# Transposing the normalised rows tile by tile instead of by the piece, in a graph transformer kernel on one core

## What is computed

```python
for i in range(4):
    h = layernorm(x) * ln1_g[i] + ln1_b[i]
    q = softmax(heads(h @ Wq[i]) * scale, axis=-1)
    k = softmax(heads(h @ Wk[i]) * scale, axis=-2)      # over all nodes
    v = heads(h @ Wv[i])
    x = x + (q @ (k^T v)) @ Wo[i] + bo[i]
    h = layernorm(x) * ln2_g[i] + ln2_b[i]
    x = x + gelu(h @ W1[i] + b1[i]) @ W2[i] + b2[i]
...
messages = relu(concat(xn[src], edge_attr) @ gnn_W1.T + gnn_b1)   # 100,000 rows, summed by dst
```

## Time and profile before

| | before |
|---|---|
| median of 3 runs | 2482.8 us (2479.87 to 2484.0) |
| the profiled execution | 2484.0 us, its span 2482.2 us |
| mean granted TensorE clock | 0.92 of full speed |
| TensorE matmul busy | 2040.7 us, 82% of the span |
| VectorE busy | 1571.9 us, 63% |
| GpSimd busy | 1318.0 us, 53% |
| ScalarE busy | 947.3 us, 38% |
| L1086 transposes | 600 |
| L830 activations | 240: 120 of 375 columns, 120 of 250 |

### The profile page before, as it was taken

The page is one execution under the profiler, slowest core; times in us unless marked ns, Lnnn a source line. Parts: engine busy times, 40 slices in busy tenths (PEclk is TensorE's granted clock), DMA queues, the critical chain, the costliest instruction groups (busy, mean ns, idle before and its releaser), DMA issues.

```text
span 2482.2 us, 36733 instructions
## 1 busy us (share of the span) xinstructions
PE 2040.7 (82%) x10686; PEld 1658.3 (67%) x10686; DVE 1571.9 (63%) x3709; ACT 947.3 (38%) x1978; POOL 1318.0 (53%) x1112
## 2 busy tenths in 40 slices
PE   3369899998889999897999988799999673999920
PEld 2247677776767777676777767677777472899920
DVE  4667777776877777677777767777776457011135
ACT  1234444443444444343444444344444241333310
POOL 3165666666556666755666665566666200332255
PEclk9779899999999999999999999999999785999965
DMA  8632222224222222422222232232223330999943
GB/s 199 198 72 57 72 69 67 68 70 116 59 70 68 69 70 68 122 59 63 71 71 70 71 102 72 60 74 68 68 69 72 71 93 21 321 331 325 326 114 95
DMA packets 262788, 260.78 MB, mean 105 GB/s; under 512 B 150233, under 2 KB 195158, under 8 KB 262674
## 3 DMA queue, kind: packets, MB, share of 16 engines
q0 software_dynamic: 124672, 132.82, 21.9%
q1 hardware_dynamic: 133890, 126.67, 16.6%
q10 hardware_dynamic: 4112, 0.03, 0.1%
HBM read 229.85 MB, written 28.39 MB: 104 GB/s over the span
## 4 chain that ended last, share of the span: by engine, by line
PE 50%; DVE 17%; POOL 11%; DMA 8%; issue 6%; ACT 5%; SPq 3%; DVEq 0%; POOLq 0%; ACTq 0%
PE bank L1040 26%; POOL G L759 10%; PE bank L1173 5%; DMA G<-P_d,src_T 4%; PE bank L1256 3%; PE bank L1264 3%; PE bank L1034 2%; PE bank L359 2%; PE bank L367 2%; PE bank L360 2%; DVE hn L1381 2%; DVE z L407 2%; DVE zl L381 2%; ACT TT L830 2%; PE bank L1100 2%
## 5 line engine op out<-in xcount | busy, mean ns | idle before, releaser
L759 POOL DMA_INDIRECT G<-P_d,src_T x896 | 1152.5, 1286 | 743.8 <-DVE z L407 457.4
L375 ACT ACTIVATE zr<-z 125x512 fp32r<-125x512 f32 x448 | 274.7, 631 | 512.9 <-DVE z L407 511.0
L407 DVE TENSOR_TENSOR z<-bank,G 125x512 f32<-125x512 f32 x448 | 294.4, 687 | 242.2 <-PE bank L367 120.5
L1173 PE MATMUL bank<-TT,W_s 128*128 128x250 f32 (+1 forms) x1280 | 367.0, 438 | 3.6 <-ACT TT L830 3.6
L1040 PE MATMUL bank<-W_s,hid 128*125 128x256 f32 x1600 | 359.6, 379 | 0.0
L1040 PEld LDWEIGHTS bank<-W_s,hid 128*125 128x125 f32 x1600 | 292.9, 188 | 42.6
L1173 PEld LDWEIGHTS bank<-TT,W_s 128*128 128x128 f32 x1280 | 241.9, 195 | 103.7 <-issue 8.9
L381 DVE SCALAR_TENSOR_TENSOR zl<-z,zr 125x512 fp32r<-125x512 f32 x448 | 289.6, 688 | 6.6 <-ACT zr L375 6.6
L359 PE MATMUL bank<-zr,onehot 125*125 125x256 f32 x896 | 270.0, 333 | 18.3 <-DVE zl L381 18.3
L360 PE MATMUL bank<-zl,onehot 125*125 125x256 f32 x896 | 229.3, 286 | 0.0
L359 PEld LDWEIGHTS bank<-zr,onehot 125*125 125x125 f32 x896 | 172.3, 192 | 44.2 <-DVE onehot L394 17.6
(11 more groups left out here) (284 smaller groups left out, 3055.5 us busy)
## 6 DMA issues: line engine op xcount, KB each, us to landing
W_s<-in_L_ffn_w SPq DMA_DIRECT2D x64, 512.0 KB, 4.3
hid<-in_L_ffn_w SPq DMA_DIRECT2D x64, 512.0 KB, 4.4
G<-P_d,src_T POOLq DMA_INDIRECT x896, 4.2
W_s<-in_L_mix_W SPq DMA_DIRECT2D x8, 1024.0 KB, 9.9
aT<-attr_d SPq DMA_DIRECT2D x224, 31.2 KB, 2.7
slot_out<-yo SPq DMA_DIRECT2D x32, 128.0 KB, 4.0
slot_out<-eT SPq DMA_DIRECT2D x32, 128.0 KB, 3.8
attr_d<-hn SPq DMA_DIRECT2D x12, 246.1 KB, 4.0
```

The source lines that it names most:

```text
L375: nc.scalar.activation(zr[:, s, k, :], z[:, k, :], ACT.Relu).then_inc(r_done, 1)
L407: nc.vector.tensor_tensor(z[:, k, :], edge_bank[k][0:ET, :], G[:, ST * s + 2 * k:ST * s + 2 * k + 2, :].rearrange("p j d -> p (j d)"), ALU ...
L759: pool.indirect_dma_start(G[:, j, :], None, P_d[:, :], bass.IndirectOffsetOnAxis(ap=src_T[:, at:at + 1], axis=0)).then_inc(g_in[j], 16)
L1173: ins = pe.matmul(to[:, 0:(b - a) * T], W1_s[:, k, part], TT[:, k, TT_PIECES[pc]], start=k == 0, stop=k == KD - 1)
```

## The change

TensorE now transposes a tile at a time: unit j of the group holds both halves of tile j, two blocks of 125 columns in one bank (`tile_T`). A group makes GT = 5 units of two transposes each instead of 4 units of three or two. ScalarE empties a unit with two activations of 125 columns, one for each half because gain and shift differ, and counts `ring_act` once, after the second. So a group has 10 activations in place of 4. The number and the shapes of the transposes stay the same, only their order changes.

The waits follow. `queries` waits for its own tile (`u + j + 2`) and no longer for a whole piece. The first part of the feed-forward block waits for b tiles of its piece (`GT + b + 1`: three, then five). The counts of units in a group (RING_GA, RING_GB, RING_M) and all positions behind them are shifted. VectorE waits for the same events under new numbers.

```diff
-        LNU = 2 * KD
-        RING_GA, RING_GB = 4 + LNU + GT, GT + LNU + 2 * NF + LNU
+        RING_GA, RING_GB = 2 * GT + 4, 3 * GT + 2 * NF
...
-            def features(u, loc, gain, shift):
-
-                for pc, (a, b) in enumerate(PC):
-                    for k in range(KD):
-                        i = KD * pc + k
-                        act.wait_ge(ring_full, u + i + 1)
-                        act.activation(TT[:, k, TT_PIECES[pc]], RING[(loc + i) % 3][:, 0:(b - a) * T], ACT.Identity,
-                                       bias=shift(k), scale=gain(k)).then_inc(ring_act, 1)
+            def features(u, loc, j, gain, shift):
+
+                act.wait_ge(ring_full, u + 1)
+                for k in range(KD):
+                    ins = act.activation(TT[:, k, tt_cols(j)], RING[loc % 3][:, 128 * k:128 * k + T], ACT.Identity,
+                                         bias=shift(k), scale=gain(k))
+                ins.then_inc(ring_act, 1)
...
-                    features(u, loc, lambda k: ln_col(0, k), lambda k: ln_col(1, k))
+                    for j in range(GT):
+                        features(u + j, loc + j, j, lambda k: ln_col(0, k), lambda k: ln_col(1, k))
...
                 def normalised(h, u, loc):
-                    for pc, (a, b) in enumerate(PC):
-                        for k in range(KD):
-                            i = KD * pc + k
-                            to = slot(u + i, loc + i)
-                            for j in range(a, b):
-                                if k == 0:
-                                    pe.wait_ge(hn_done, h + j + 1)
-                                ins = pe.transpose(to[:, (j - a) * T:(j - a) * T + T], hn[:, j, 128 * k:128 * k + 128], ident[0:T, 0:T])
-                            ins.then_inc(ring_full, 1)
+                    for j in range(GT):
+                        pe.wait_ge(hn_done, h + j + 1)
+                        tile_T(u + j, loc + j, hn[:, j, :])
...
                     for j in range(GT):
-                        pe.wait_ge(ring_act, u + (KD + 1 if j < PC[0][1] else LNU + 1))
+                        pe.wait_ge(ring_act, u + j + 2)
                         row(r + j, rloc + j, [(TT[:, k, tt_cols(j)], Wq_s[:, k, :]) for k in range(KD)])
...
                             if f == 0:
-                                pe.wait_ge(ring_act, u0 + (GT + KD * pc + KD + 1))
+                                pe.wait_ge(ring_act, u0 + (GT + b + 1))
```

More of the change, by code:

```diff
@@ L342, in build @@
         EG_B = EG_M + 1
-        RING_M, ROW_M = LNU + NG * RING_GA, NG * ROW_GA
+        RING_M, ROW_M = GT + NG * RING_GA, NG * ROW_GA
         RING_B, ROW_B = RING_M + 1, ROW_M + GT + KD
@@ L877, in _ @@
                     eg = l * EG_L + g + (EG_FIRST + EG_A)
-                    u0, q0 = l * RING_L + g * RING_GA + (RING_A + LNU), l * (2 * NG) + g * 2
+                    u0, q0 = l * RING_L + g * RING_GA + (RING_A + GT), l * (2 * NG) + g * 2
                     for pc, (a, b) in enumerate(PC):
@@ L887, in _ @@
                     for j in range(GT):
-                        copy_tile(u0 + LNU + 4 + j, LNU + 4 + j, es[:, j, :].rearrange("p (k n) -> p k n", k=KD), 128, T)
+                        copy_tile(u0 + GT + 4 + j, GT + 4 + j, es[:, j, :].rearrange("p (k n) -> p k n", k=KD), 128, T)
                     edges(eg, 1)
@@ L907, in second @@
                     std(std5b[:, :], mv5b[:, :, 1], b_std)
-                    features(u0 + GT, GT, lambda k: ln_col(2, k), lambda k: ln_col(3, k))
+                    for j in range(GT):
+                        features(u0 + GT + j, GT + j, j, lambda k: ln_col(2, k), lambda k: ln_col(3, k))
                     step(0)
@@ L911, in second @@
                         for pc, (a, b) in enumerate(PC):
-                            loc = GT + LNU + 2 * f + pc
+                            loc = 2 * GT + 2 * f + pc
                             act.wait_ge(ring_full, u0 + loc + 1)
@@ L918, in second @@
                     if not last:
-                        normalised(u0 + GT + LNU + 2 * NF, GT + LNU + 2 * NF)
+                        normalised(u0 + 2 * GT + 2 * NF, 2 * GT + 2 * NF)
                     step(5)
@@ L1092, in _ @@
                     h0, q0 = l * HN_L + g * GT + (NT + GT), l * (2 * NG) + g * 2
-                    u0, r0 = l * RING_L + g * RING_GA + (RING_A + LNU), l * ROW_L + g * ROW_GA + ROW_A
+                    u0, r0 = l * RING_L + g * RING_GA + (RING_A + GT), l * ROW_L + g * ROW_GA + ROW_A
                     for pc, (a, b) in enumerate(PC):
@@ L1108, in _ @@
                         for j in range(a, b):
-                            loc = LNU + 4 + j
+                            loc = GT + 4 + j
                             pe.wait_ge(ring_act, u0 + (2 * pc + 3))
@@ L1120, in _ @@
                                 if h == 0:
-                                    pe.wait_ge(ring_act, u0 + (LNU + 4 + j + 2))
+                                    pe.wait_ge(ring_act, u0 + (GT + 4 + j + 2))
                                     pe.wait_ge(row_dve, r0 + j + 2)
@@ L1139, in _ @@
                 pe.wait_ge(wQ_in, l * 32 + 32)
-                queries(uM - GT - LNU, rM, 0)
+                queries(uM - GT, rM, 0)
                 pe.wait_ge(ring_act, uM + 2)
@@ L1163, in second @@
                     step(0)
-                    normalised(h0, u0 + GT, GT)
+                    for j in range(GT):
+                        pe.wait_ge(hn_done, h0 + j + 1)
+                        tile_T(u0 + GT + j, GT + j, hn[:, j, :])
                     for f in range(NF):
@@ L1178, in second @@
                     if not last:
-                        normalised(h0 + GT, u0 + GT + LNU + 2 * NF, GT + LNU + 2 * NF)
-                        queries(u0 + GT + LNU + 2 * NF, r0 + GT, GT)
+                        normalised(h0 + GT, u0 + 2 * GT + 2 * NF, 2 * GT + 2 * NF)
+                        queries(u0 + 2 * GT + 2 * NF, r0 + GT, GT)
                     step(5)
-                    pe.wait_ge(ring_act, u0 + (GT + LNU + 2 * NF + 1))
+                    pe.wait_ge(ring_act, u0 + (2 * GT + 2 * NF + 1))
                     for j in range(GT):
@@ L1428, in first @@
                     eg = l * EG_L + g + (EG_FIRST + EG_A)
-                    u0, r0, q0 = l * RING_L + g * RING_GA + (RING_A + LNU), l * ROW_L + g * ROW_GA + ROW_A, l * (2 * NG) + g * 2
+                    u0, r0, q0 = l * RING_L + g * RING_GA + (RING_A + GT), l * ROW_L + g * ROW_GA + ROW_A, l * (2 * NG) + g * 2
                     dve.wait_ge(ring_full, u0)
@@ L1533, in second @@
                     if not last:
-                        dve.wait_ge(ring_full, u0 + GT + LNU)
+                        dve.wait_ge(ring_full, u0 + 2 * GT)
                         normalised(g + 1)
```

## The result

The changed kernel takes 2508.5 us (median of 4 runs, 2503.6 to 2511.3), the kernel before 2482.6 us beside it: ratio 1.0102, 95% interval 1.0088 to 1.0116. It is slower by 25.9 us, where 38.2 was forecast; the time lies in the range of 2499 to 2560 us. The profiled execution took 2506.9 us (span 2504.1), 22.9 more than the profiled one of before.

What follows compares the result with a forecast made beforehand. The prediction took the first loop's chain to run around all engines, with ScalarE's activations of `TT` on it. The terms 25.2 + 8.0 + 2.4 + 2.3 + 0.3 = 38.2 us gave 2521.0 us, range 2499 to 2560.

Steps and rivals of the forecast that it cites:

- The first loop: 20 passes: `TT` ends later on ScalarE, delaying `zr`, `es` and the transposes behind them 1.26 us each; 25.2 us.
- the layer's start: 4 places where TensorE's slow transposes, not ScalarE, set the time; 0.1 us each, 0.3 us.
- The next queries: 16 passages: the first query matmul stands behind all five units and starts 0.50 us later; 8.0 us.
- The second norms: 20 places: hidden behind gathers in 14, 0.4 us each in 6 (2.4 us), plus two more lowered clocks (2.3 us).
- the middle: Each layer's stretch from its last group's context updates to the second norm's first `hn`; the sum had no term for it.
- Faster by the early start: Rival: activations under about 0.2 us let queries and six norms start sooner; 12 us less, 2471 us; chance 0.05.
- The loop's delay: Rival: a wait of VectorE or for V absorbs it, leaving only queries and norms; 2494 us; chance 0.09.
- The clock did not fall in first-loop passes: Rival: TensorE's clock falls in ten of 20 first-loop passes, and behind the other second norms; 2550 us; chance 0.14.

Runs made afterwards that it cites:

- only_c: The kernel before with the change made in the first loop alone; 2497.7 us, ratio 1.0056.
- one_act: The changed kernel with one activation of 250 columns per unit, using the first half's gain and shift for both; 2492.6 us, ratio 1.0041.
- split10: The kernel before with its four units, each emptied by one activation for each of its tiles, ten in all; 2525.0 us, ratio 1.0169.
- only_b: The kernel before with the change made before the next queries alone; 2490.5 us, ratio 1.0032.
- only_a: The kernel before with the change made at the second norms alone; 2481.1 us, ratio 0.9985.
- late_tile: The changed kernel with the first loop's transposes moved behind the context matmuls and its activations behind the second `zr`; 2526.0 us, ratio 1.0168.

## Why the prediction was right, and where it was off

**The first loop** (forecast 25.2 us, with the layer's start 25.5) measured 21.1, the layer's start included. The mechanism was right step by step: the fourth and fifth units wait for ScalarE, the edge products come 0.82 us later (0.81 forecast), `zr` and `es` follow, and no gap of the loop gives it back. only_c shows the place, one_act and split10 the number of activations as its main part. The size was off: I put 1.26 us on a pass and it was 1.09. The sum also took 1.16 us for the two `zr`, where the row has 1.23; read rightly, it would have been 1.33 us a pass, further off. The transposes behind `es` came 1.19 us later, and the activations of `TT` end sooner (3.58 instead of 3.66 us), so a neighbour is hidden by more than the 111 ns that I had from the long forms: (3.58 - 0.476) / 9 = 345 ns held, 131 ns overlapped. By this row the Trainium skill's price (ScalarE: Activation LUTs, section What ACT_TABLE_LOAD costs) agrees in the length, 476 ns, and not in the 93 ns of overlap here.

**The next queries** (8.0) start 0.47 us later behind the activations, against 0.50. The first product then took 0.09 us less, so that 0.38 us each, 6.1 us in all, reached the first `qm`. only_b's +8.4 comes near the forecast 8.0 only with the four falls of the clock that it holds. That a query waits only for its own tile gave nothing, as forecast: it stands behind all the transposes.

**The second norms** (2.4 + 2.3). The first matmul is 0.43 us later, forecast 0.4. Stretches with a lowered clock behind a norm went from 8 to 11, where I expected about 10, but three of them were longer than any before. These are stretches of the changed kernel, with the granted clock before the last two columns:

```profile
351.50:358.50 7.00, 6.38 (x19) 3.77 (x17) 4.00 (x8) 6.59 (x15) 4.60 (x4) 0.57 0.20 43
867.00:872.00 5.00, 4.41 (x12) 2.60 (x13) 3.46 (x7) 4.98 (x12) 3.44 (x3) 0.66 0.17 34
```

The first is almost all at 1.2 GHz for 7 us, and that group took 32.0 us to its queries instead of 29.3; the second is the usual case (30.5 us).

Together queries and norms were forecast at 12.7 us and measured 10.8 + 2.3 = 13.1 us. That these agree is luck: the queries' part is 6.1 us instead of 8.0, and the norms' is 4.7 + 2.3 = 7.0 instead of 4.7. Nor do the norms cost what was forecast. At full clock there is no delay: nine stretches of the changed kernel reach the queries' activations 26.64 us after the norm on average, ten of before after 26.76. (only_a has 0.3 us of the forecast 0.4, in its stretches with a lowered clock.) The norms' loss is the clock, above all the three long falls, whose stretches reach the activations after 29.0 to 29.1 us.

**What failed is the sum's silence about the middle.** The touched parts cost 34.2 of the 38.2 us forecast, but the middle was 7.6 us shorter, and the sum had no term for it: it looked for gaps that give time back inside the loop alone. (The end, which the change doesn't touch, was 4.8 us shorter.) A stretch of the second layer's middle, before and then after:

```profile
701.00:727.00 26.00, 17.26 (x71) 13.17 (x71) 17.77 (x36) 6.88 (x12) 15.03 (x13) 0.80 0.33 86
```

```profile
710.00:736.00 26.00, 17.66 (x82) 13.58 (x81) 19.32 (x41) 6.89 (x12) 14.00 (x12) 0.87 0.35 87
```

The granted clock is higher, and the 26 us hold more of the middle's work (82 matmuls against 71). Over the four middles the clock was at 1.2 GHz for 47.8 us before and for 34 after. Counting the time at the lower level, a middle takes in most profiles some 28 us with about 7 us at 1.2 GHz, 30 with about 10, and 32 with about 14. The kernel before had two of 32 us in its profiled execution; eight of the ten experiments' profiles have 115 to 121 us in all, six of them near 120. So about 3.6 of the 7.6 us were one execution's, and 4 us remain that also show in only_c. With 34.2 - 4 = 30 us the measured 22 to 26 us (2508.5 against the medians of before in all calls, 2482.6 to 2486.1) is still some 4 to 8 us lower; that rest is not settled. The gap of VectorE ahead of a middle's second `z`, which in the kernel before is a wait for a gather, also shrank, by 2.2 us over the four layers. But split10 has as short gaps there, 10 us at 1.2 GHz in each middle, and 119.9 us for the four: the shorter middle goes with the clock, and what moved the clock was not found.

**The rivals.** Faster by the early start did not come: ScalarE is held 0.345 us by an activation of 125 columns, far above 0.2. The loop's delay was not taken up inside the loop. The clock did not fall in first-loop passes of the changed kernel (0 of 16), though it did in late_tile. For what the Trainium skill describes (TensorE: Matmul & The Clock Gate, section A second HAM failure mode: psum-queue depth-cycling), the traces decide nothing: late_tile's falls inside the loop stand at the keys' wait for `TT`, which is one wait of 1.74 us in all 16 passes while the clock fell in five, and split10, which waits longer at the ring than the changed kernel (0.71 us against 0.34 + 0.26), has no fall behind a norm.

## What to carry to other kernels

Cutting a transfer into smaller units so that it can start sooner can pay if the engine that empties them takes time by the column. ScalarE did not: an activation of 125 columns cost 476 ns against 662 for 375, and ten held ScalarE 3.58 us instead of 2.12. Look at what stands behind the emptying on that engine, and at how many units the ring takes before its reader is the bound. The gain lay not in a finer unit but in its place: the half that the next consumer needs stayed early, the other half went behind the work that was waiting for ScalarE, and the kernel took 0.9% less. Moving all of it late made the kernel 0.5% slower.

## What was not expected of the hardware

TensorE's clock made a stretch of equal work take distinct lengths: a layer's middle 28, 30 or 32 us, its start 28.6 us in only_a and 30.7 before, a second norm to the queries 29.3, 30.4 or 32.0 us in the changed kernel. The falls come after quiet stretches: ahead of a norm's TensorE waited some 1.14 us for `hn`, in the middle 2.4 to 3.6 us. But it waited 1.12 to 1.16 us ahead of all 20 norms in both kernels, and the clock fell behind 8 and 11 of them. Which ones it was changed from kernel to kernel, and nothing here tells why. The tile form at the second norms alone had a lowered clock behind 16 norms of 20 instead of 8, and a higher one in all four layers' starts; why was not settled. Effects of single edits measured by whole-kernel times so don't add to better than some 8 us here, while the same edits' stretches (first loops 441.0 and 440.6 us, in only_c and in the changed kernel) repeat within half a microsecond.
